# Expert tiles add their rows into the residual in DRAM with accumulating scatters, one reload replaces two pick buffers, and two weight units are split earlier

## The reference

```python
    x = x + _L1_gnn_ref(xn, ...) + _L1_mix_ref(xn[None], ...)[0]
    x = x + _L1_ffn_ref(_layernorm(x, axis=-1)[None], ...)[0]
    xn = _layernorm(x, axis=-1)
    x = x + _L2_gnn_ref(xn, ...) + _L2_mix_ref(xn[None], ...)[0]
```

## Time and profile before

| | us |
|---|---|
| runs, median of 3 (lowest to highest) | 3866.82 (3859.94 to 3867.56) |
| time of the profiled execution | 3863.52 |
| its span | 3861.8 |
| PE busy | 3385.8 (88%) |
| DVE busy | 1821.3 (47%) |
| POOL busy | 952.4 (25%) |
| ACT (ScalarE) busy | 992.1 (26%) |

### The profile page before, as it was taken

One profiled execution on the slowest core, in us unless ns is written; L12 is line 12 of the kernel. 1 busy time (PEld: TensorE's weight loads), 2 busy tenths in 40 slices (PEclk: granted clock), 3 DMA queues, 4 the chain that ended last, 5 costly groups with the idle time before them and its releaser, 6 DMA issues. The chain is left out here.

```text
span 3861.8 us, 45010 instructions
## 1 busy us (share of the span) xinstructions
PE 3385.8 (88%) x17342; PEld 2037.8 (53%) x17342; DVE 1821.3 (47%) x3276; ACT 992.1 (26%) x2135; POOL 952.4 (25%) x1140
## 2 busy tenths in 40 slices
PE   3878999899999898799959599949988988799898
PEld 2543567555567554455446367735664444345454
DVE  6753335635334722664162532243555667631544
ACT  0211145422235422211133234410223221100221
POOL 2000426276335344322032011120311000101132
PEclk9998999899899898899979699979998999899899
DMA  1002224133123141010000189960100000000001
GB/s 66 1 9 71 72 63 131 47 112 102 64 79 113 62 126 49 30 35 32 1 28 22 66 343 416 416 199 0 36 34 17 33 33 28 17 17 17 17 33 43
DMA packets 122181, 297.13 MB, mean 77 GB/s; under 512 B 16391, under 2 KB 49703, under 8 KB 106626
## 3 DMA queue, kind: packets, MB, share of 16 engines
q1 hardware_dynamic: 117660, 280.11, 20.7%
q0 software_dynamic: 4320, 14.27, 0.9%
HBM read 242.29 MB, written 52.04 MB: 76 GB/s over the span
## 5 line engine op out<-in xcount | busy, mean ns | idle before, releaser
L1942 POOL TENSOR_SCALAR raw<-raw 128x512 f32<-128x512 f32 x356 | 237.7, 668 | 2401.8 <-PE ps L342 935.7
L342 PE MATMUL ps<-ARENA,units 128*128 128x500 f16 (+1 forms) x4104 | 747.2, 344 | 46.7 <-POOL units L1946 20.1
L354 PE MATMUL ps<-units,ARENA 128*125 128x512 f16 x3360 | 742.8, 383 | 10.7 <-DVE ARENA L1258 5.3
L354 PEld LDWEIGHTS ps<-units,ARENA 128*125 128x125 f16 x3360 | 457.2, 138 | 291.2 <-DVE X L1647 16.5
L342 PEld LDWEIGHTS ps<-ARENA,units 128*128 128x128 f16 x4104 | 402.1, 98 | 390.7 <-issue 26.6
L1246 DVE TENSOR_TENSOR ARENA<-tmp,ARENA 128x500 f16<-128x500 f32 (+2 forms) x310 | 212.1, 688 | 489.8 <-ACT ARENA L956 331.6
L955 ACT ACTIVATE tmp<-ps,cols 128x500 f32<-128x500 f32 (+1 forms) x252 | 161.1, 639 | 624.1 <-PE ps L342 617.1
L310 PE MATMUL ps<-ident,ARENA 125*128 125x125 f32 x640 | 130.6, 363 | 209.0 <-DVE ARENA L1258 87.9
L1946 POOL TENSOR_TENSOR units<-raw,units 128x512 f16<-128x512 f32 x228 | 278.1, 1220 | 19.3
L377 PE MATMUL ps<-ARENA,AT 125*125 125x512 f32 x600 | 258.2, 592 | 2.6 <-DVE ARENA L1384 1.7
L447 PE MATMUL ps<-proj,ARENA 128*125 128x512 f32 x480 | 247.8, 628 | 3.7 <-ACT ARENA L1041 2.6
(11 more groups left out here) (350 smaller groups left out, 4274.0 us busy)
## 6 DMA issues: line engine op xcount, KB each, us to landing
ARENA<-split_d SPq DMA_DIRECT2D x108, 1024.0 KB
raw<-in_units SPq DMA_DIRECT2D x228, 256.0 KB, 2.5
raw<-in_moe SPq DMA_DIRECT2D x128, 256.0 KB, 3.4
split_d<-AT SPq DMA_DIRECT2D x128, 256.0 KB, 2.8
units<-in_units SPq DMA_DIRECT2D x10, 1024.0 KB, 4.7
adj_d<-AT SPq DMA_DIRECT2D x1, 5468.8 KB
AT<-adj_d SPq DMA_DIRECT2D x1, 5468.8 KB
ARENA<-picks_d SPq DMA_DIRECT2D x4, 896.0 KB
```

Of the source, the lines that this page charges most:

```text
L342: ins = pe.matmul(o[:, 0:nt * R], wt, mv_, start=(i == 0), stop=(i == len(steps) - 1))
L354: ins = pe.matmul(o[0:R, :], th(srcT, h, k, t, 1), w(k, g), start=(i == 0), stop=(i == len(steps) - 1))
L1942: pool.tensor_scalar(r, r, WEIGHT_SCALE, 1.0, ALU.mult, ALU.mult).then_inc(sem("pool_step"), 1)
```

## The change

It does four things.

1. Output of the experts. DRAM buffer `x_d` takes the place of `picks_d`. SP stores X (with the expert biases already in) into it, behind the seventh ring load (L2087 of the changed kernel). POOL's 27 scatters now add to the rows in DRAM (`compute_op=ALU.add`). Two tiles may hold the same row, so each scatter first waits until the one before it has landed, the first one until X is stored.
2. Reload. SP reads `x_d` back into X in 6 DMAs instead of 12, and `with_picks` does no additions, only the layer norm.
3. Indices. The slot map carries one column per tile instead of two, with one memset and one DVE operation less in `ranks` and `slots`.
4. Order. POOL and SP call `routed_experts` at `GATE_UNIT + 2`, so units 38 and 39 are loaded and split ahead of it. SP's check on rows is moved along.

```diff
-picks_d = nc.dram_tensor("picks_d", (2 * PICK + TILES * B, D), F32, kind="Internal").ap()
+x_d = nc.dram_tensor("x_d", (N + TILES * B, D), F32, kind="Internal").ap()
...
-                    ins = pe.matmul(o[:, 0:2 * TILES], on_part[:, i, :], on_tile[:, i, :, :], start=(i == 0), stop=(i == 2 * T - 1))
+                    ins = pe.matmul(o[:, 0:TILES], on_part[:, i, :], on_tile[:, i, :], start=(i == 0), stop=(i == 2 * T - 1))
...
-                step(ins)
-                step(dve.memset(on_tile[:, 0:T, 1, :], 0.0), "one_hots")
+                step(ins, "one_hots")
...
-                step(dve.tensor_copy(slot_sb, o[:, 0:2 * TILES]), "slots_read")
...
-                step(stt(slot_c, slot_sb[:, TILES:2 * TILES], float(PICK), slot_sb[:, 0:TILES], ALU.mult, ALU.add))
-                step(stt(pick_i, slot_c, -1.0, slot_z, ALU.add, ALU.add), "slots")
+                step(dve.tensor_copy(slot_sb, o[:, 0:TILES]), "slots_read")
...
+                step(stt(pick_i, slot_sb, -1.0, slot_z, ALU.add, ALU.add), "slots")
...
-            def add_picks(after):
+            def with_picks(after):
                 for c, (t0, nt) in enumerate(CH):
-                    dve.wait_ge(sem(f"picks_back{c}"), 16 * 2 * len(PARTITION_CUTS))
+                    dve.wait_ge(sem(f"x_back{c}"), 16 * len(PARTITION_CUTS))
                     for t in range(t0, t0 + nt):
-                        tt(nat(X, t), nat(X, t), nat(back[0], t), ALU.add).then_inc(sem("dve_step"), s.one("dve_step"))
-                        dve.wait_ge(*s.latest())
-                        tt(nat(X, t), nat(X, t), nat(back[1], t), ALU.add).then_inc(sem("dve_step"), s.one("dve_step"))
-                        dve.wait_ge(*s.latest())
                         after(t)
...
                     pool.wait_ge(sem("tile_y"), g + 1)
-                    pool.indirect_dma_start(picks_d, bass.IndirectOffsetOnAxis(ap=pick_i[:, g:g + 1], axis=0), tile_y[g % 2], None)\
-                        .then_inc(sem(f"picks_stored{g % 2}"), 16)
+                    if g == 0:
+                        pool.wait_ge(sem("x_stored"), 16 * len(PARTITION_CUTS))
+                    else:
+                        pool.wait_ge(sem(f"picks_added{(g - 1) % 2}"), 16 * ((g - 1) // 2 + 1))
+                    pool.indirect_dma_start(x_d, bass.IndirectOffsetOnAxis(ap=pick_i[:, g:g + 1], axis=0), tile_y[g % 2], None, compute_op=ALU.add)\
+                        .then_inc(sem(f"picks_added{g % 2}"), 16)
...
-                if u == GATE_UNIT:
+                if u == GATE_UNIT + 2:
                     routed_experts()
...
                         i += 1
+                        if i == RING_SLOTS:
+                            sp.wait_ge(sem("moe_bias"), marks["L1_bias"])
+                            for p0, p1 in PARTITION_CUTS:
+                                sp.dma_start(x_d[0:N, :].rearrange("(t p) d -> p t d", p=R)[p0:p1],
+                                             X[p0:p1, :].rearrange("p (t d) -> p t d", t=T)).then_inc(sem("x_stored"), 16)
...
                 for c, (t0, nt) in enumerate(CH):
-                    for k in range(2):
-                        for p0, p1 in PARTITION_CUTS:
-                            sp.dma_start(back[k][p0:p1, t0 * D:(t0 + nt) * D].rearrange("p (t d) -> p t d", t=nt),
-                                         picks_d[k * PICK + t0 * R:k * PICK + (t0 + nt) * R, :].rearrange("(t p) d -> p t d", p=R)[p0:p1])\
-                                .then_inc(sem(f"picks_back{c}"), 16)
+                    for p0, p1 in PARTITION_CUTS:
+                        sp.dma_start(X[p0:p1, t0 * D:(t0 + nt) * D].rearrange("p (t d) -> p t d", t=nt),
+                                     x_d[t0 * R:(t0 + nt) * R, :].rearrange("(t p) d -> p t d", p=R)[p0:p1]).then_inc(sem(f"x_back{c}"), 16)
...
-                if u == GATE_UNIT:
+                if u == GATE_UNIT + 2:
                     while rows_sent <= ROWS.index("E1"):
```

More of the change, by code:

```diff
@@ L65 @@
 ROW_W = D + NE
-PICK = 1280
 RING_SLOTS = 7
@@ L212, in build @@
         tile_f, part_f = (K[0:R, 4760 + 20 * i:4780 + 20 * i] for i in range(2))
-        slot_sb = K[:, 4800:4854]
-        slot_z, slot_c = K[:, 4854:4881], K[:, 4881:4908]
+        slot_sb, slot_z = K[:, 4800:4827], K[:, 4854:4881]
         first_row = K[0:R, 4908:4916]
         on_part = K[0:R, 2500:3780].bitcast(F16).rearrange("p (i n) -> p i n", n=B)
-        on_tile = K[0:R, 3780:4320].bitcast(F16).rearrange("p (i c g) -> p i c g", c=2, g=TILES)
+        on_tile = K[0:R, 3780:4050].bitcast(F16).rearrange("p (i g) -> p i g", g=TILES)
         ring = [ARENA[:, i * 2048:(i + 1) * 2048].bitcast(F16).rearrange("p (g k n) -> p g k n", g=2, k=KC) for i in range(RING_SLOTS)]
@@ L224, in build @@
         tile_y = [Y[:, 4112 + i * D:4112 + (i + 1) * D] for i in range(2)]
-        back = [ARENA[:, (2 + i) * T * D - T * D:(3 + i) * T * D - T * D] for i in range(2)]
         unit_release = []
@@ L1522, in ranks @@
                     ts(on_part[:, i, :], iota128[0:R, :], part_f[:, i:i + 1], None, ALU.is_equal)
-                step(tt(on_tile[:, :, 1, :], tile_f.unsqueeze(2).to_broadcast([R, 2 * T, TILES]), iota27[0:R, :].unsqueeze(1).to_broadcast([R, 2 * T, TILES]), ALU.is_equal))
+                step(tt(on_tile, tile_f.unsqueeze(2).to_broadcast([R, 2 * T, TILES]), iota27[0:R, :].unsqueeze(1).to_broadcast([R, 2 * T, TILES]), ALU.is_equal))
                 for k in range(2):
-                    ins = tt(on_tile[:, k * T:(k + 1) * T, 0, :], on_tile[:, k * T:(k + 1) * T, 1, :], tok1[0:R, :].unsqueeze(2).to_broadcast([R, T, TILES]), ALU.mult)
-                step(ins)
-                step(dve.memset(on_tile[:, 0:T, 1, :], 0.0), "one_hots")
+                    ins = tt(on_tile[:, k * T:(k + 1) * T, :], on_tile[:, k * T:(k + 1) * T, :], tok1[0:R, :].unsqueeze(2).to_broadcast([R, T, TILES]), ALU.mult)
+                step(ins, "one_hots")
             def slots():
@@ L1535, in slots @@
                 o = s.bank("dve")
-                step(dve.tensor_copy(slot_sb, o[:, 0:2 * TILES]), "slots_read")
-                step(ts(gather_i, slot_sb[:, 0:TILES], -1.0, 0.0, ALU.add, ALU.max))
-                step(stt(slot_z, slot_sb[:, 0:TILES], 0.0, pad_rows, ALU.is_equal, ALU.mult))
-                step(stt(slot_c, slot_sb[:, TILES:2 * TILES], float(PICK), slot_sb[:, 0:TILES], ALU.mult, ALU.add))
-                step(stt(pick_i, slot_c, -1.0, slot_z, ALU.add, ALU.add), "slots")
+                step(dve.tensor_copy(slot_sb, o[:, 0:TILES]), "slots_read")
+                step(ts(gather_i, slot_sb, -1.0, 0.0, ALU.add, ALU.max))
+                step(stt(slot_z, slot_sb, 0.0, pad_rows, ALU.is_equal, ALU.mult))
+                step(stt(pick_i, slot_sb, -1.0, slot_z, ALU.add, ALU.add), "slots")
             def routed_experts():
@@ L1568, in routed_experts @@
                         if g >= 3:
-                            dve.wait_ge(sem(f"picks_stored{(g - 1) % 2}"), 16 * ((g - 1) // 2))
+                            dve.wait_ge(sem(f"picks_added{(g - 1) % 2}"), 16 * ((g - 1) // 2))
                         ts(tile_y[(g - 1) % 2], o[:, :], w_tab[:, g - 1:g], WS, ALU.mult, ALU.mult).then_inc(sem("tile_y"), s.one("tile_y"))
-            def add_picks(after):
+            def with_picks(after):
                 for c, (t0, nt) in enumerate(CH):
-                    dve.wait_ge(sem(f"picks_back{c}"), 16 * 2 * len(PARTITION_CUTS))
+                    dve.wait_ge(sem(f"x_back{c}"), 16 * len(PARTITION_CUTS))
                     for t in range(t0, t0 + nt):
-                        tt(nat(X, t), nat(X, t), nat(back[0], t), ALU.add).then_inc(sem("dve_step"), s.one("dve_step"))
-                        dve.wait_ge(*s.latest())
-                        tt(nat(X, t), nat(X, t), nat(back[1], t), ALU.add).then_inc(sem("dve_step"), s.one("dve_step"))
-                        dve.wait_ge(*s.latest())
                         after(t)
@@ L1809, in _ @@
             row_free("E1")
+            marks["L1_bias"] = s.sent["moe_bias"]
             routed_experts()
-            add_picks(lambda t: ln_tile(X, M, "xn", t))
+            with_picks(lambda t: ln_tile(X, M, "xn", t))
             dve.wait_ge(*s.latest())
@@ L1961, in routing_constants @@
                 pool.iota(jtab, pattern=[[B, T]], base=0, channel_multiplier=0, allow_small_or_imprecise_dtypes=True)
-                pool.iota(pad_rows, pattern=[[B, TILES]], base=2 * PICK + 1, channel_multiplier=1, allow_small_or_imprecise_dtypes=True)
+                pool.iota(pad_rows, pattern=[[B, TILES]], base=N + 1, channel_multiplier=1, allow_small_or_imprecise_dtypes=True)
                 pool.iota(tok1, pattern=[[R, T]], base=1, channel_multiplier=1, allow_small_or_imprecise_dtypes=True)
```

3 lines of the change are left out of this document (1 added, 2 removed).

## The result

The changed kernel takes 3893.06 us (median of 4 runs, 3888.47 to 3894.92), the kernel before in the same session 3863.57 us (4 runs, 3859.94 to 3867.56): a ratio of 1.0074, 95% interval 1.0057 to 1.0092. It is slower. The forecast was 3884 with a range of 3856 to 3916, and slower was its likeliest case. The profiled execution took 3892.5 us with a span of 3890.7; before, the span was 3861.8.

The account below looks back on a forecast made before the run. PE and the DMA engines were taken as both full in the experts' stage, with PE idle around it. Tiles ending 43.4 us later less 25.6 of tail give +17.8 on 3863.5, plus 3.3 for the median: 3884 us, range 3856 to 3916.

Parts of the forecast that it names:

- The head: Ahead of the tiles: SP's stores queue behind L2bout, which waits for "moe_bias"; PE starts tiles 25 us later.
- Unit 38's split: In the head: POOL's split beside DVE's additions slows DVE by 3 us, bounds 0 and 8 x 0.9.
- The stores: In the head, on SP: from release to POOL's first gather, L2bout, Y and gate weights take 13.4 us.
- The gather: End of the head: issue 0.3 us, then 8.2 us to land; bounds 3.3 and 10.0.
- The tiles: Experts' stage: the DMA engines' bill sets their end, at 2585.3, 43.4 us later than before.
- one more pass of the same bytes: In the tiles: 27 adding scatters must fetch the old rows, 17 us more on the DMA engines.
- the bill: In the tiles: ring loads, gathers and scatters 305.8 us, X's store 8.1, second pass 17, counted from 2248.9.
- PE's own pace: In the tiles: if PE keeps its 307.6 us after the late start, the tiles end at 2567.0.
- The tail: Last scaling to layer 2's first large product: one reload, no additions or splits; 32.9 us, 25.6 us less.
- the engines have room: Rival, tiles: 417 GB/s is PE's pace, so the second pass is absorbed; 3866 to 3871, no change; chance 0.25.
- The short head: Rival, head: PE starts 16 us late, not 25, and the addition is hidden; -10 us, 3857; chance 0.17.
- The slow chain: Rival, tiles: each scatter waits for the one before, period 13.1 us, stage 52 us longer; 3920; chance 0.15.

Follow-up runs that it names:

- b1_order_alone: The kernel before with only units 38 and 39 moved ahead of the experts on POOL and SP; 3880.8 us, ratio 1.0036.
- a1_rows_late: The changed kernel with SP's row loads behind E1 (L2gb2, L2bout) held back until the experts are issued; 3885.6 us, ratio 1.0055 to before.
- a2_plain: The changed kernel with plain scatters instead of adding ones, all waits kept, experts' sum left out; 3872.3 us, ratio 1.0019 to before.
- a3_gather_ahead: The changed kernel with every gather issued one tile sooner on POOL; 3889.9 us, ratio 1.0060 to before.
- b2_adds_alone: The changed kernel without the new order: units 38 and 39 split behind the tiles as before; 3880.3 us, ratio 1.0033 to before.
- c3_before_gather: The kernel before with nothing but the gathers issued one tile sooner; 3862.9 us, ratio 1.0001.
- d1_late38: The changed kernel with row loads held behind the experts, gathers one tile sooner, unit 38's POOL split held until DVE's layer norm `Y` and `L1_lo` finish; 3864.5 us.

## Why the prediction was right, and where it was off

**The head** was forecast at +25.0 and measured +27.7, by the mechanism named: SP held at L2bout behind "moe_bias". b1_order_alone shows it with nothing else changed, a1_rows_late takes it away. But part of the nearness is luck. This execution reached the stage early: L1768 starts at 2139.90, L1777 before at 2143.24, and other executions have that start anywhere from 2139.2 to 2148.1. Counted from there to the first transposes the head is 122.2 us long against 91.1, so it cost 31.1 us, 6 more than forecast. Unit 38's split cost DVE 4.2 us (I took 3), and all of it is still there when the slot map starts (77.3 us after that start against 73.1); on the clock of the span it reads as 0.8 us only because of the early start. The bias matmuls took 17.43 us instead of 14.40, at the lower clock. The stores took 14.7 us from the release to the first gather's issue (13.7 forecast); in them the gate weights, which I let hide behind Y's for all but 1.5 us, cost SP 3.98 us, and the ring moved at 2253.3, not 2248.9. The gather landed after 8.8 us (8.2).

**The tiles** were forecast 18.4 us longer and measured 23.4. The term "one more pass of the same bytes", 17 us, was right to size: 13.7 to 16.1. The rest of the bill is some 4 us larger than worked out: from the ring's first load to the last scaling a2_plain, without additions, took 323.8 us against my 319.4, and the changed kernel 339.8 against my 336.4. I had also let 6.8 us of the bill hide behind PE's own pace (2567.0 against 2560.2 without store and second pass). None of it hid: b1_order_alone, with the late head alone, has tiles of 307.4 us, and on it the store of X and the additions stand in full, 8.2 and 16.1 us, which gives the changed kernel's 331.7. What I had wrong is who waits. I had PE wait for `split_d`; it waited 0.9 us for it and 21.9 us for gathered rows. A gather needed 9.9 us behind an addition's 1.59 us of issue, where I had costed neither. In this kernel that costs little, since the engines' bill is as long (a3_gather_ahead); with the head repaired it is worth about 17 us (340.7 against 323.9). I had seen this place only as the rival of a chain from addition to addition. That chain didn't hold: additions landed 9.8 us after issue, inside the period of 12.06.

**The tail** was forecast at 32.9 us and measured 34.4: to the reload 5.5 (4.6), the first chunk 6.8 (7.0), the norm 14.0 (14.0), to the product 8.1 (7.3). b1_order_alone confirms the 8 us for POOL's splits (7.4), as long as the additions are there.

**The rivals.** That the engines have room is refuted by a2_plain: at a share of 1.02 they moved 417 GB/s beside a PE that waited for weights. My argument for it, the share of 1.02, was weak: b2_adds_alone shows 1.01 at 381 GB/s. The figure of 435 GB/s, which the Trainium skill gives in "DMA: Bandwidth & Descriptors", section "Where 436 GB/s comes from", was not reached in any window quoted here. The short head fell with the 24 us that PE waited. The slow chain fell as said.

**The sum**: +17.8 forecast, +28.9 in the profile. The difference is 2.7 (head), 5.0 (tiles), 1.5 (tail) and 1.9 behind the tail, of which I had said nothing. The head's 2.7 are 6.1 too little forecast less 3.3 of early start; 3.0 of the 6.1 are the bias matmuls at the lower clock. The 1.9 at the end may be the execution's too: a2_plain, with the same code behind the tail, has 1261.3 there. The median (3893) came nearer to the forecast (3884) than the profile to its sum, and by luck: I had added 3.3 us for the median of three runs before, and with the fourth run that median is 3863.57. From there the change cost 29.5 us, where the sum had 17.8.

## What to carry to other kernels

Before moving a block of work on an in-order queue, list everything that is issued between its old and its new place, waits included: here one 0.25 MB row load with a late semaphore moved Y's stores, the gate weights and the ring's first load back by some 38 us (the ring from 2215.42 in a1_rows_late to 2253.29), and the repair, done carelessly, made another row late, worth some 7 us. After a repair compare every stage with the kernel before, and not only the stage repaired: from a1_rows_late on the "rest" column showed that loss.

Where DMA engines are full, moving an addition into the DMA isn't free. Weigh what it removes (here a reload of 1.0 MB per chunk and 20 DVE additions in a stretch where PE waits, 17 us of tail once the order is the same) against what it adds (one more pass of the scattered bytes and a store of X, 18 to 20 us of tiles). Here the two came out even.

## What the runs showed of the hardware

- An accumulating scatter of 128 rows of 2 KB costs full DMA engines 0.5 to 0.6 us more than a plain one, the moved rate falls from 417 to 398 GB/s, its issue on POOL takes 1.59 us instead of 0.99, and it lands later. The DMA issues of 2588 to 2612 in the changed kernel show the last two, with no ring load beside them, at a median of 4.8 us where a plain one took 2.7:

```profile
x_d<-ARENA,proj POOLq DMA_INDIRECT x2, 4.8
```

- The same 20 matmuls, on the same inputs, took 14.05 to 14.40 us in three executions and 17.42 to 17.43 in eleven, by when the granted clock rose. The kernel before and c3_before_gather, which share their code up to there, stand on either side.
- A DMA share near 1 goes with different rates: 417 GB/s at 1.02 with plain scatters, 398 at 1.03 with additions, and 381 at 1.01 where PE waits for the gathers.
- POOL and DVE slow each other. L1768 took 10.92 us beside POOL's split instead of 6.71, and 6.72 again where the split was held back (d1_late38); L1772, which began at 2150.85 when POOL was through, took its 6.11 as before. POOL's own L1938 took 1.47 us beside L1768, and 1.15 in the quarter before it (2137.79).
